# Attention: what prepares the next batch stands one head earlier, and a projection stands between the turn and the use of the score maxima

## What is computed

```
xn = _rms_norm(x, g_norm) * (1.0 + scale) + shift
qkv = xn @ W_qkv
q = _rms_norm(q, g_q)
k = _rms_norm(k, g_k)
logits = jnp.einsum('bhqd,bhkd->bhqk', q, k) * d ** (-0.5)
attn = jax.nn.softmax(logits, axis=-1)
o = jnp.einsum('bhqk,bhkd->bhqd', attn, v)
o = jnp.swapaxes(o, 1, 2).reshape(b, n, dim)
return o + o @ W_out
```

## Time and profile before

| what | value |
| --- | --- |
| median of 3 runs | 1795.61 us (1793.72 to 1798.26) |
| the profiled execution's own time | 1789.96 us |
| its span | 1788.2 us |
| attention, first to last turn of maxima | 1156.16 to 1513.44 us |
| TensorE's granted clock, mean | 0.901 |

### The profile page before, as it was taken

One profiled execution on the slowest core, in us unless ns is written; L12 is line 12 of the kernel. 1 busy time (PEld: TensorE's weight loads), 2 busy tenths in 40 slices (PEclk: granted clock), 3 DMA queues, 4 the chain that ended last, 5 costly groups with the idle time before them and its releaser, 6 DMA issues. The chain is left out here.

```text
span 1788.2 us, 76589 instructions
## 1 busy us (share of the span) xinstructions
PE 1593.9 (89%) x32043; PEld 1222.2 (68%) x32043; DVE 1184.0 (66%) x4252; ACT 911.5 (51%) x3320; POOL 601.9 (34%) x1805
## 2 busy tenths in 40 slices
PE   6999999999999999997399974788888887799999
PEld 5999999999999999997266642355555555544444
DVE  5778888887877778887744427565666676573231
ACT  5555555555555556555245445366666677432130
POOL 0333333333333333333445434143333333580000
PEclk9999999999999999655599985798989889799999
DMA  5110101111100111101447444000000000130001
GB/s 173 45 31 11 50 20 41 29 29 40 49 25 5 34 45 46 37 22 57 150 130 252 132 145 145 35 1 1 2 2 1 2 1 2 42 100 23 26 0 48
DMA packets 45735, 90.76 MB, mean 51 GB/s; under 512 B 6736, under 2 KB 25296, under 8 KB 45392
## 3 DMA queue, kind: packets, MB, share of 16 engines
q1 hardware_dynamic: 38992, 64.89, 11.6%
q0 software_dynamic: 6400, 20.98, 3.5%
HBM read 66.90 MB, written 18.87 MB: 48 GB/s over the span
## 5 line engine op out<-in xcount | busy, mean ns | idle before, releaser
L402 PE MATMUL bank<-arena 128*128 128x8 f16 x12288 | 501.2, 170 | 9.7 <-issue 5.1
L405 PE MATMUL bank<-arena 128*128 128x16 f16 x12288 | 496.8, 182 | 3.1 <-issue 2.2
L402 PEld LDWEIGHTS bank<-arena 128*128 128x128 f16 x12288 | 412.0, 97 | 39.1 <-ACT bank L498 19.1
L405 PEld LDWEIGHTS bank<-arena 128*128 128x128 f16 x12288 | 412.3, 97 | 4.3 <-issue 3.2
L664 POOL TENSOR_TENSOR arena<-arena 128x16 f32<-128x16 f32 x512 | 116.8, 228 | 542.7 <-DVE arena L607 527.9
L468 ACT ACTIVATE arena<-arena 128x16 f32<-128x16 f32 x512 | 114.6, 224 | 307.0 <-DVE arena L586 306.7
L597 DVE TENSOR_TENSOR_SCAN arena<-arena,bank 128x64 f32<-128x64 f32 x512 | 147.1, 287 | 19.4 <-ACT arena L468 2.5
L586 DVE TENSOR_REDUCE arena<-bank 128x16 f32<-128x48 f32 x512 | 100.2, 196 | 84.4 <-PE bank L405 79.3
L1958 PE MATMUL bank<-arena 128*128 128x512 f16 x704 | 152.3, 379 | 1.7 <-PEq L1461 1.7
L375 PE MATMUL bank<-arena 128*128 128x256 f16 x1008 | 148.6, 274 | 1.6 <-issue 1.6
L1496 PE MATMUL bank<-arena 128*128 128x512 f16 x576 | 142.7, 402 | 4.5 <-DVE arena L1752 4.5
(11 more groups left out here) (202 smaller groups left out, 2752.5 us busy)
## 6 DMA issues: line engine op xcount, KB each, us to landing
arena<-yrows SPq DMA_DIRECT2D x16, 512.0 KB, 4.2
arena<-in_wgu SPq DMA_DIRECT2D x48, 128.0 KB, 2.2
arena<-in_xT SPq DMA_DIRECT2D x32, 128.0 KB, 2.2
hrows<-arena SPq DMA_DIRECT2D x16, 256.0 KB, 4.0
arena<-in_xtok SPq DMA_DIRECT2D x16, 256.0 KB, 8.9
out_y<-arena SPq DMA_DIRECT2D x16, 256.0 KB, 2.0
arena<-in_wih SPq DMA_DIRECT2D x4, 768.0 KB, 6.4
arena<-in_whh SPq DMA_DIRECT2D x4, 768.0 KB, 5.4
```

The source lines that it names most:

```text
L402: mm = nc.tensor.matmul(dst[:, j * B:(j + 1) * B, 1], w, h[:, 0], start=home not in opened, stop=False, skip_group_check=True)
L405: mm = nc.tensor.matmul(dst[:, j * B:(j + 1) * B, 1:3], w, h.rearrange("p a c -> p c a"), start=home not in opened, stop=False, skip_group ...
```

## The change

The tables of the loop move the preparation of the next batch one head ahead. P0 of the batch after the next one leaves the head loop: it stands between `turn_max` and `turn_out(b, 3)`, ahead of the first two `scores_t`, so the projections of a batch stand at heads 0 to 5 without a P0, and `scores` of head 15 stand ahead of the last `values`. For that, `xn` has to be ready before the batch ends: ScalarE makes the high half in two halves at heads 9 and 10, and GpSimd makes the low half in four quarters between its `low_p` of heads 10 to 13. VectorE makes a low half of `xn` for batch 0 alone. At the end of a batch `turn_max` and `high_v` on ScalarE, and `low_v` on VectorE, stand ahead of the last `high_out` and `low_out`.

```diff
-        PROJECT_AT = {0: 0, 1: 1, 2: 2, 3: 3, 5: 4, 6: 5}
-        ROOT_AT = 4
-        NORM_AT = {4: (0,), 5: (1, 2, 3)}
...
-        STACK_AT = {8: (0,), 9: (1,), 10: (2,), 13: (3,)}
-        MAX_AT = {9: (0, 1), 10: (2, 3), 11: (4, 5, 6), 12: (7, 8), 13: (9, 10), 14: (11, 12), 15: (13, 14)}
+        PROJECT_AT = {0: 1, 1: 2, 2: 3, 4: 4, 5: 5}
+        SQUARES_AT = {1: (0, 1), 2: (2,), 3: (3,)}
+        ROOT_AT = 3
+        NORM_AT = {3: (0,), 4: (1, 2, 3)}
...
+        STACK_AT = {7: (0,), 8: (1,), 9: (2,), 13: (3,)}
+        MAX_AT = {8: (0, 1), 9: (2, 3), 10: (4, 5, 6), 11: (7, 8), 12: (9, 10), 13: (11,), 14: (12, 13), 15: (14, 15)}
+        NORM_X_AT = {9: 0, 10: 1}
...
                     if not last:
-                        scores(b + 1, 15)
+                        turn_max(b + 1)
+                        if b + 2 < B:
+                            project(b + 2, 0)
                     turn_out(b, 3)
                     if not last:
-                        turn_max(b + 1)
                         scores_t(b + 1, 0)
                         scores_t(b + 1, 1)
...
                 turn_max(0)
+                project(1, 0)
                 scores_t(0, 0, True)
...
                     softmax(b, 0)
+                    if not last:
+                        take_out(b + 1, 0)
                     for h in range(H):
                         if h + 1 < H:
                             softmax(b, h + 1)
+                        if more and h in NORM_X_AT:
+                            norm_x(b + 2, NORM_X_AT[h])
...
-                    high_out(b, 3)
                     if not last:
                         turn_max(b + 1)
                         high_v(b + 1)
-                    if more:
-                        norm_x(b + 2)
+                    high_out(b, 3)
...
                     normalise(b, 3)
                     if not last:
-                        maximum(b + 1, 15)
+                        low_v(b + 1)
                     low_out(b, 3)
-                    if not last:
-                        low_v(b + 1)
-                    if more:
-                        norm_x(b + 2)
...
+                def norm_low(b, k):
+                    pool.wait_ge(xn_hi, 2 * b + k // 2 + 1)
+                    G.tensor_tensor(xn[:, 1, k, :], xnf[:, b, k, :], xn[:, 0, k, :], ALU.subtract).then_inc(xn_lo, 1)
...
                     for h in range(POOL_LOW, H):
                         low_p(b, h)
+                        if b + 2 < B and 10 <= h < 10 + KT:
+                            norm_low(b + 2, h - 10)
```

More of the change, by code:

```diff
@@ L1413, in mixed_net_kernel @@
         POOL_LOW = 8
-        PROJECT_AT = {0: 0, 1: 1, 2: 2, 3: 3, 5: 4, 6: 5}
-        ROOT_AT = 4
-        NORM_AT = {4: (0,), 5: (1, 2, 3)}
[L1418 to L1421, removed]
-        STACK_AT = {8: (0,), 9: (1,), 10: (2,), 13: (3,)}
-        MAX_AT = {9: (0, 1), 10: (2, 3), 11: (4, 5, 6), 12: (7, 8), 13: (9, 10), 14: (11, 12), 15: (13, 14)}
+        PROJECT_AT = {0: 1, 1: 2, 2: 3, 4: 4, 5: 5}
+        SQUARES_AT = {1: (0, 1), 2: (2,), 3: (3,)}
+        ROOT_AT = 3
+        NORM_AT = {3: (0,), 4: (1, 2, 3)}
+        SPLIT_AT = {4: (0, 1), 5: (2, 3)}
+        LOW_AT = {5: (0, 1), 6: (2, 3)}
+        OUT_AT = {3: 0, 6: 1}
+        O2_AT = {6: (0,), 7: (1,)}
+        STACK_AT = {7: (0,), 8: (1,), 9: (2,), 13: (3,)}
+        MAX_AT = {8: (0, 1), 9: (2, 3), 10: (4, 5, 6), 11: (7, 8), 12: (9, 10), 13: (11,), 14: (12, 13), 15: (14, 15)}
+        NORM_X_AT = {9: 0, 10: 1}
         vzero = sem("vzero")
@@ L1446, in wait_low, with xn_half, xnf_half @@
                 eng.wait_ge(pool_low, (H - POOL_LOW) * b + h - POOL_LOW + 1)
+        def xn_half(part, half):
+            return xn[:, part, 2 * half:2 * half + 2].rearrange("p k s -> p (k s)")
+        def xnf_half(b, half):
+            return xnf[:, b, 2 * half:2 * half + 2].rearrange("p k s -> p (k s)")
         def xnf_of(b):
@@ L1483, in project @@
                     if i == 0:
-                        pe.wait_ge(xn_lo, b + 1)
+                        pe.wait_ge(xn_lo, KT * (b + 1))
                     if i < 2 and not first:
@@ L1599, in batch @@
                         if h == 0 and not last:
-                            project(b + 1, 0)
+                            project(b + 1, PROJECT_AT[0])
                         if h + 2 < H:
@@ L1644, in _, with norm_x @@
                 A = nc.scalar
-                def norm_x(b):
-                    A.activation(xn[:, 0].rearrange("p k s -> p (k s)"), xnf_of(b), ACT.Copy).then_inc(xn_hi, 1)
+                def norm_x(b, half):
+                    A.activation(xn_half(0, half), xnf_half(b, half), ACT.Copy).then_inc(xn_hi, 1)
                 def take_out(b, i):
@@ L1726, in batch @@
                             high_o2(b, jp)
-                norm_x(0)
+                norm_x(0, 0)
+                norm_x(0, 1)
                 for i in range(4):
@@ L1735, in _ @@
                     high_qk(0, n)
+                norm_x(1, 0)
+                norm_x(1, 1)
                 for g in range(4):
@@ L1739, in _ @@
                 high_v(0)
-                norm_x(1)
                 for b in range(B - 2):
@@ L1750, in norm_x @@
                 def norm_x(b):
-                    dve.wait_ge(xn_hi, b + 1)
-                    V.tensor_tensor(xn[:, 1].rearrange("p k s -> p (k s)"), xnf_of(b),
-                                    xn[:, 0].rearrange("p k s -> p (k s)"), ALU.subtract).then_inc(xn_lo, 1)
+                    for half in range(2):
+                        dve.wait_ge(xn_hi, 2 * b + half + 1)
+                        V.tensor_tensor(xn_half(1, half), xnf_half(b, half), xn_half(0, half),
+                                        ALU.subtract).then_inc(xn_lo, KT // 2)
                 def sum_squares(b, i):
@@ L1827, in batch @@
                         if not last:
-                            if 0 < h < 5:
-                                sum_squares(b + 1, h - 1)
+                            for i in SQUARES_AT.get(h, ()):
+                                sum_squares(b + 1, i)
                             if h == ROOT_AT:
@@ L1918, in _ @@
                     squares(0, i)
+                for k in range(KT):
+                    norm_low(1, k)
                 for b in range(B - 1):
```

## The result

The changed kernel takes 1776.9 us (median of four runs, 1776.51 to 1779.41), the kernel before beside it 1795.3 us. The ratio is 0.990, with a 95% interval of 0.988 to 0.992. It is faster by 18.4 us, twice the 9.1 us of the forecast, and inside the range of 1773 to 1802.

A forecast was written before the change was run, and what follows sets the result against it. TensorE bounds the first stretch of a batch, VectorE the second. Seven batches sum to 48.9 + 250.0 + 49.3 = 348.2 us against 357.3, minus 9.1, so 1786.5 us against the median; range 1773 to 1802.

The forecast's parts named there:

- P0 in the gap, and the way to P3: First stretch, turn of maxima to first stacking: P0 fills the DMA gap; P3 ends at 12.54 us, before 17.37.
- The chain behind P3 grows by 1.0: From P3's end to the first stacking, ScalarE and VectorE work takes 1.0 us longer net, 15.2 against 14.20.
- Rival D: ScalarE's chain from P3 to the stacking grows by the whole boundary gain; 0 to 3 us left, 1794; chance 0.08.
- The second stretch at the upper clock, 19.4: From first stacking to next turn: 18.18 us before, 19.4 with more ScalarE work, at the upper clock.
- ScalarE's stalls: Second stretch: VectorE's low_out waits for ScalarE's longer queue, plus 0.9 us at the first and 0.5 at the second.
- I expect the lower clock there in each batch, at 2.3 us.: At the waits before the second stacking, TensorE drops to its lower clock in every batch, costing 2.3 us.
- The clock at the turn, one in three, 0.6 per batch: At the turn of the maxima, the lower clock one time in three at 1.7 us, so 0.6 per batch.
- GpSimd's quarters at nothing: GpSimd's four norm_x quarters at heads 10 to 13 take 0.65 us each, 2.6 together, and cost no time.
- Rival E: GpSimd's quarters take 1.7 to 1.8 us each and delay values and P0: 1809 us, slower; chance 0.14.
- Rival B: The upper clock holds in the middle of each batch: 16 us more gain, 1770.5 us; chance 0.10.
- Rival C: The lower clock everywhere, 2.65 us in each middle and 1.7 at each turn: 1796.8 us, no change; chance 0.20.
- forecast A: The summed forecast itself: 1786.5 us, 1779 to 1794 by the clock's bounds; chance 0.48.

The follow-up runs named there:

- e3_p0_behind: The changed kernel with P0 alone moved back behind the first two scores_t of the next batch: 1808.7 us.
- e4_gap_only: The kernel before with P0 moved into the gap and norm_x early, the tables of the heads as before: 1792.4 us.
- e2_low_order: The changed kernel with VectorE's low_p of head 7 behind the last two low_qk instead of ahead of them: 1772.9 us.
- e8_nx_late: The changed kernel with norm_x later, ScalarE's halves at heads 11 and 12 and GpSimd's quarters behind them, no filled waits: 1774.7 us.
- the second trace: The changed kernel run and profiled again unaltered: 1778.7 us.
- e10_order_nx_fill: The changed kernel with low_p of head 7 behind low_qk, norm_x later, and discarded matmuls before both stackings and in heads 14 and 15: 1753.25 us.
- e11_order_fill: The same as e10_order_nx_fill, but with norm_x early again, at heads 9 and 10: 1764.6 us.
- e7_fill_nx: The changed kernel with seven discarded matmuls in each of TensorE's two stacking waits, and norm_x later, at heads 11 and 12: 1765.0 us.

## Why the prediction came out half as large

- **P0 in the gap, and the way to P3.** Right: 27.70 us for the first stretch, as forecast; the DMA is hidden in all but one batch. `e3_p0_behind` (32.6) and `e4_gap_only` (29.03) met the same sum.
- **The chain behind P3 grows by 1.0.** Right, and `e2_low_order` shows the cause. Rival D fell with it.
- **The second stretch at the upper clock, 19.4.** Right in kind, 0.35 too high: 19.07, and in part by luck. ScalarE's stalls were 0.53 and 0.41, not 0.9 and 0.5: VectorE has two copies and not one ahead of its first `low_out`, so it comes later too. The 0.35 for the fourth copy was under 0.1. Against that, VectorE waited 2.12 us for `high_o2` where it had waited 1.55, which the sum left out.
- **"I expect the lower clock there in each batch, at 2.3 us."** This is the step that failed, by its size. The lower clock came in every batch, but beside ScalarE's stall it cost 1.1 us as a rule and 1.4 in the mean of batches 1 to 5. The prediction took its 2.3 from stretches of the kernel before, which had no stall to hide it, and added it to one as if both were paid one after the other. The overlap is one half of the miss: without the stall the clock costs 1.7. The other half is that 1.7 itself lies below 2.3. Why the kernel before paid 2.65 at 0.82 and `e8_nx_late` 1.7 at 0.83 was not tried. Of the 9.2 us by which the sum of the batches missed, second stretches of 20.5 instead of 21.7 us in batches 1 to 5 make 5.9, and that of batch 6 makes 1.2; the turns make 1.8 (next point).
- **The clock at the turn, one in three, 0.6 per batch.** In the first trace it never fell there, which saved the 3.6 us put down for batches 1 to 6; late DMAs took 1.8 of them back, 1.6 in batch 1. In the second trace it fell twice in six. Over the eight traces of kernels with P0 in the gap and no filling in the last heads it had fallen at 20 of 48 turns, at 1.2 to 1.8 us each. One in three was near it, and the first trace was lucky. But the reason that the prediction gave was not right: the idle gap was not what lowered the clock. In the kernel before it fell 0.3 to 0.7 us ahead of the turn in four of batches 1 to 6, still in the last heads, as here in batch 3:

```profile
1308.99:1309.69 0.70, 0.24 (x2) 0.20 (x2) 0.70 (x2) 0.00 (x0) 0.00 (x0) 1.00 0.00 0
1309.71:1310.05 0.34, 0.23 (x2) 0.00 (x0) 0.29 (x1) 0.08 (x1) 0.00 (x0) 0.50 0.00 0
```

  That fits `e10_order_nx_fill` and `e11_order_fill`, whose matmuls stand in those heads: from batch 1 on the clock fell at none of their turns.
- **GpSimd's quarters at nothing.** Right inside the batches: 0.67 us each (16.1 us in 24, mean 671 ns), for 0.65 taken; `values` 15 wait 0.33 us for the last low half. Rival E fell. Not seen: the four quarters of batch 1, which stand beside VectorE's `low_qk` of batch 0, and which cost the first batch 0.9 us (last section).
- **Rival B**, the upper clock in the middle, did not come by itself. With filled waits it did, and was worth 1.1 or 1.7 us a batch, not the 2.3 that it had. **Rival C** fell. The rule that it took from the Trainium skill, "TensorE: Matmul & The Clock Gate", PE-mode transpose, that transposes do not count as TensorE activity, can't be told from the changed kernel, where the clock fell in each second stretch; in `e7_fill_nx`, with the waits filled, stretches with 64 transposes kept 1.00 in batches 2 to 6.
- What the sum left out: the DMA that lands late in one or two batches of seven. And forecast A's own range, 1779 to 1794, was too narrow at its low end: 1.31 for 2.3 in six middles and no fall at six turns make 1777, which is what was measured.

## What to carry to other kernels

Two delays found in different kernels or in different places of a timeline must not be added before asking whether they overlap: here a slow TensorE gave ScalarE time to empty its queue, and did so only where the clock fell ahead of the stall. When a change moves work on one engine into another's gap, try each half by itself: here one alone lost 13.7 us, and the other gave nothing that could be measured. And where the clock falls in short waits next to sparse work, matmuls whose products are thrown away, put into those waits, cost nothing on the path, and gave 12 us here (1765.0 to 1753.3).

## What was not expected of the hardware

The DMA of the maxima landed late in some batches. TensorE's wait in batch 1 of the changed kernel, and the DMA queues around it from 1208 to 1214 us (packets, MB, share):

```profile
1209.15 1.14 SPq L1477 DMA_DIRECT2D arena<-arena  x2
...
1213.05 0.61 PE L1560 MATMUL bank<-arena 97*128 97x256 f16 x4 [1.42 <-DMA arena<-arena]
...
q8 instruction: 1, 0.02, 1.1%
q1 hardware_dynamic: 64, 0.01, 0.9%
```

From issue to first use it took 3.90 us, where 2.34 were needed before. In eight of the ten traces of kernels with P0 in the gap TensorE waited for it at one or two turns, 0.7 to 1.6 us each. The traces show what came with it: one packet of 16 KB, 0.9 to 1.4 us long, of the queue that the profile calls `instruction`; around the turn of batch 2, which saw no wait, there is none. Of the 104 turns in the thirteen traces the second DMA landed more than 3.15 us after the turn at 18, and at each of these 18 such a packet ended between 1.9 and 3.6 us after the turn, at none of the 86 others. In the kernel before, the packet of batches 1 and 3 started 4.05 us after the turn, when the maxima had landed (3.0). So the change moved such a packet onto the transfer. That the packet holds the transfer up is argued from this; no run moved it.

VectorE was slowed by GpSimd. When GpSimd's four quarters of batch 1 ran beside VectorE's last `low_qk` of batch 0, which copy and subtract from SBUF to SBUF:

```profile
1138.43 0.29 DVE L1790 COPY arena<-arena 128x512 f16<-128x512 f16 x1
1138.63 0.68 DVE L1791 TENSOR_TENSOR arena<-arena 128x512 f16<-128x512 f32 x1
...
1138.93 3.29 POOL L1911 TENSOR_TENSOR arena<-arena 128x256 f16<-128x256 f32 x4 [6.73 <-ACT arena L1657]
1139.23 0.76 DVE L1790 COPY arena<-arena 128x512 f16<-128x512 f16 x1
1139.91 1.15 DVE L1791 TENSOR_TENSOR arena<-arena 128x512 f16<-128x512 f32 x1
```

The same copy took 0.76 instead of 0.29 us and the same subtraction 1.15 instead of 0.68, and the quarters 0.82 each instead of 0.67. The Trainium skill, "SBUF — State Buffer", who interferes with whom, says that a VectorE instruction with two SBUF inputs and a GpSimd one that reads SBUF keep each other out, the one that started first blocking the other. The rows agree as far as both queues lost, each behind the other in turn; the copy, which has one SBUF input and lost 0.47 us, would come under its other condition, a VectorE mode that takes both ports; no row here shows the mode. The prediction had used the rule for GpSimd alone, and not asked what its quarters do to VectorE.
